# Routed mixture of experts: scale arithmetic from GpSimd to VectorE, a sequence prepared every six tile steps, the next tile's weight address read behind the present up product

## What is computed

```python
def _L1_ffn_ref(x, w_gate, w1, w3, w2):
    xt = x.reshape(-1, embed_dim)
    logits = xt @ w_gate                                # 8 experts
    top_logits, sel = jax.lax.top_k(logits, 2)
    probs = jax.nn.softmax(top_logits, axis=-1)
    h = silu(einsum('td,edh->eth', xt, w1)) * einsum('td,edh->eth', xt, w3)
    y = einsum('eth,ehd->etd', h, w2)                   # H = 256
    yk = y[sel.T, t_idx[None, :], :]                    # the two chosen experts of each token
    return einsum('ktd,tk->td', yk, probs)
...
x = x + _L1_ffn_ref(_layernorm(x), w_gate, w1, w3, w2)
```

## Time and profile before

| | before |
|---|---|
| median of 3 runs | 2675.16 us (2672.88 to 2677.55) |
| the profiled execution's own time | 2669.71 us |
| its span, first to last instruction | 2667.5 us |
| granted TensorE clock, mean | 0.894 |
| busy: PE, DVE, ACT, POOL | 2200.5 (82%), 1647.1 (62%), 1278.4 (48%), 1448.1 us (54%) |
| the two routed layers | from about 1545 to 1845, and from 2364 to 2667.5 us of the span |

### The profile page before, as it was taken

How to read it: one execution, slowest core, us unless ns; L and a number is a source line. 1 busy time by engine, 2 the same in 40 slices (tenths; PEclk the granted TensorE clock), 3 DMA queues, 4 the chain that set the end, 5 groups by cost and what they waited for, 6 DMA issues and landing times. The chain is left out here.

```text
span 2667.5 us, 40619 instructions
## 1 busy us (share of the span) xinstructions
PE 2200.5 (82%) x11840; PEld 1315.8 (49%) x11840; DVE 1647.1 (62%) x4376; ACT 1278.4 (48%) x2252; POOL 1448.1 (54%) x1499
## 2 busy tenths in 40 slices
PE   4577997998779889989999945776999999954766
PEld 3345564666656556644444433544444444433544
DVE  6865775776667657756666633435787787733424
ACT  4642454332435433336666523432677677642433
POOL 5923654443256533446666655744676666535743
PEclk8687898998979999989999957887999999966888
DMA  1001111222011122210000032232000000021224
GB/s 49 0 3 29 37 37 50 83 86 82 1 41 37 25 90 96 88 62 1 1 1 1 1 89 62 59 92 79 0 1 1 1 0 1 1 77 51 67 69 133
DMA packets 106948, 112.44 MB, mean 42 GB/s; under 512 B 21816, under 2 KB 86200, under 8 KB 106488
## 3 DMA queue, kind: packets, MB, share of 16 engines
q1 hardware_dynamic: 97656, 91.08, 11.6%
q0 software_dynamic: 9088, 18.89, 2.2%
HBM read 71.91 MB, written 25.29 MB: 36 GB/s over the span
## 5 line engine op out<-in xcount | busy, mean ns | idle before, releaser
L2330 DVE TENSOR_REDUCE l_diffneg_max<-psum 128x1 fp32r<-128x512 f32 x512 | 335.5, 685 | 92.7 <-PE psum L2068 86.6
L2245 ACT ACTIVATE l_diffweights<-psum 128x1024 f32<-128x1024 f32 x256 | 262.0, 1026 | 128.9 <-PE psum L2097 127.9
L2068 PE MATMUL psum<-l_diffkz,l_diffQ 128*128 128x512 f32 (+1 forms) x512 | 235.2, 478 | 3.2 <-DVE l_diffneg_max L2330 2.1
L5034 POOL DMA_INDIRECT results<-l_moe1y,l_moe1xt x156 | 151.8, 973 | 149.1 <-DVE l_moe1y L4944 129.6
L2869 ACT ACTIVATE l_lightswapped<-psum 32x512 f32<-32x512 f32 x304 | 179.0, 589 | 101.1 <-DVE l_lightturned L2961 97.7
L1595 DVE TENSOR_REDUCE l_attn0neg_max<-psum 128x1 fp32r<-128x512 f32 x256 | 167.2, 683 | 54.0 <-PE psum L1329 51.3
L4710 PE MATMUL psum<-l_moe1w,l_moe1zt 128*128 x312 | 186.2, 681 | 9.1 <-ACT l_moe1zt L4790 6.3
L1501 ACT ACTIVATE l_attn0weights<-psum 128x1024 f32<-128x1024 f32 x128 | 130.2, 1023 | 120.7 <-PE psum L1351 120.6
L174 POOL TENSOR_TENSOR settled<-powers 128x1 f32<-128x1 f32 x113 | 27.5, 244 | 294.1 <-DVE l_alibimv L701 69.6
L1722 POOL TENSOR_TENSOR l_attn0half_sums<-l_attn0weights 128x2048 f32<-128x2048 f32 x30 | 137.1, 4571 | 89.6 <-ACT l_attn0weights L1501 89.6
L4294 ACT ACTIVATE l_moe0s<-psum 128x512 f32<-128x512 f32 x144 | 85.8, 596 | 198.4 <-PE psum L854 173.9
(11 more groups left out here) (606 smaller groups left out, 6109.8 us busy)
## 6 DMA issues: line engine op xcount, KB each, us to landing
l_moe0bcs<-gate_rows SPq DMA_DIRECT2D x64, 512.0 KB, 4.4
l_moe1xt<-sorted SPq DMA_DIRECT2D x156, 66.0 KB, 1.8
l_attn0Q<-l_attn0q_hi SPq DMA_DIRECT2D x128, 64.0 KB
l_moe1yb<-results SPq DMA_DIRECT2D x32, 256.0 KB, 3.3
l_moe1w<-in_moe_w SPq DMA_DIRECT2D x6, 1024.0 KB, 8.3
l_attn0Q<-l_attn0q_lo SPq DMA_DIRECT2D x64, 64.0 KB
l_moe0w_raw<-in_moe_w SPq DMA_DIRECT2D x20, 128.0 KB, 4.7
results<-l_moe1y,l_moe1xt POOLq DMA_INDIRECT x156, 2.2
```

The source lines that it names most:

```text
L2068: nc.tensor.matmul(ps[:, bank, :], Q[rows, n % 4, st * P:(st + 1) * P], kz[rows, n % 4, hh, :], start=True, stop=True).then_inc(pe_max.sem ...
L2245: nc.scalar.activation(weights[:, tt, 2 * pair:2 * pair + 2, :], ps[:, S[m % 2]:S[m % 2] + 2, :], ACT.Exp, scale=SCALE).then_inc(act_exp.s ...
L2330: nc.vector.tensor_reduce(neg_max[:, n % 2, st, row:row + 1], ps[:, bank_of(("max", n, b)), :], AXX, ALU.max, negate=True).then_inc(vec_ma ...
L5034: p.indirect_dma_start(core.dram["results"], bass.IndirectOffsetOnAxis(ap=xt[:, n % SLOTS, R.DEST:R.DEST + 1].bitcast(U32), axis=0), y[:, ...
```

## The change

- `APART` is 6 in place of 8: a sequence every six steps. The chunk's sizes become tuples, with the same values (4 and 4 sequences), and loops over them are rewritten; a last empty turn is dropped.
- GpSimd's `token_scale` keeps the power only. VectorE adds epsilon to the variance behind the statistics (with a settling memset ahead) and makes the shift in a step of its own (`shifted`); variance, scale and shift get two buffers each. Sequence 0 takes the scale that the layer before left (`open_scale`) without GpSimd.
- `destinations` goes from GpSimd's two iotas per sequence to one iota for all at the layer's start and a cast on VectorE in `weighted`.
- On TensorE the address of tile i + 1 is read behind `up` of tile i.

```diff
-    SEQS = 4
...
+    SEQS = (4, 4)
...
-    APART, SPAN = 8, 10
+    APART, SPAN = 6, 10
...
-        TURNS = range(R.TILES + 3)
+        prepare_steps = lambda c: range(APART * (R.SEQS[c] - 1) + SPAN + 4)
+        turns = lambda c: range(R.TILES[c] + 2)
...
-                at_w = {}
+                at_w = {0: expert_of(0)}
                 tile_turned(n0)
                 tile_turned(n0 + 1)
-                for i in TURNS:
-                    if i < R.TILES:
-                        at_w[i] = t.value_load(table[0:1, c, W_AT + i:W_AT + i + 1], min_val=0, max_val=7 * R.COLS)
+                for i in turns(c):
+                    if i < R.TILES[c]:
                         up(n0 + i, at_w[i])
-                    if 0 <= i - 2 < R.TILES:
+                    if i + 1 < R.TILES[c]:
+                        at_w[i + 1] = expert_of(i + 1)
+                    if 0 <= i - 2 < R.TILES[c]:
                         down(n0 + i - 2, at_w.pop(i - 2))
...
             def tokens(j):
                 act_z.start()
-                wait(a, pool_scale, j, "shift")
+                wait(a, vec_shift, j, "shift")
                 if j >= 2:
                     rows_sorted(a, j - 2)
...
+                wait(d, vec_stats, j, "mean", NQ - 1)
+                settle(core, d)
+                wait(d, pool_scale, j - 2, "scale")
+                inc(v.tensor_scalar(var[:, j % 2, :], mv[:, j % 2, :, 1], LN_EPS, None, ALU.add), "var")
+
+            def shifted(j):
+                vec_shift.start()
+                if j:
+                    wait(d, pool_scale, j, "scale")
+                wait(d, act_z, j - 2, "again")
+                v.scalar_tensor_tensor(shift[:, j % 2, :], moments(j)[:, :, 0], -1.0, scale_of(j)[:, :], ALU.mult, ALU.mult
+                                       ).then_inc(vec_shift.sem, vec_shift.step("shift"))
...
+                inc(v.tensor_copy(rows[:, j % 2, :, :, R.DEST].bitcast(U32), dest[:, :, j, :]), "to")
...
+                if due(c, k, 1) is not None:
+                    shifted(due(c, k, 1))
...
+            nc.gpsimd.iota(dest[:, :, :, :].rearrange("p k j q -> p (k j q)"), [[P, 2 * NSEQ * NQ]], 0, 1).then_inc(counted, 1)
...
             def token_scale(j):
                 pool_scale.start()
...
-                if j:
-                    wait(p, vec_stats, j, "mean", NQ - 1)
-                wait(p, act_z, j - 1, "again")
-                settle(core, p)
-                inc(nc.gpsimd.tensor_scalar(minus[:, :], moments(j)[:, :, 0], -1.0, None, ALU.mult), "minus_mean")
-                inc(nc.gpsimd.tensor_scalar(var[:, :], moments(j)[:, :, 1], LN_EPS, None, ALU.add), "var")
-                wait_for("var")
-                inc(nc.gpsimd.tensor_tensor(scale[:, :], var[:, :], core.half, ALU.pow), "scale")
-                wait_for("scale")
-                inc(nc.gpsimd.tensor_tensor(shift[:, :], minus[:, :], scale[:, :], ALU.mult), "shift")
...
+                wait(p, vec_stats, j, "var")
+                wait(p, vec_shift, j - 2, "shift")
+                wait(p, act_z, j - 2, "again")
+                nc.gpsimd.tensor_tensor(scale[:, j % 2, :], var[:, j % 2, :], core.half, ALU.pow
+                                        ).then_inc(pool_scale.sem, pool_scale.step("scale"))
```

More of the change, by code:

```diff
@@ L13 @@
 from contextlib import ExitStack
+from itertools import accumulate
 import math
@@ L4554, in routed_block @@
         stats, mv = sb("stats", [P, NQ, 6]), sb("mv", [P, 2, NQ, 2])
-        minus, var, scale, shift = sb("minus", [P, NQ]), sb("var", [P, NQ]), sb("scale", [P, NQ]), sb("shift", [P, NQ])
+        var, scale, shift = sb("var", [P, 2, NQ]), sb("scale", [P, 2, NQ]), sb("shift", [P, 2, NQ])
         rows = sb("rows", [P, 2, 2, NQ, R.WIDTH])
@@ L4562, in routed_block @@
         count, whole, tiles_i, tiles, ends = sb("count", [P, 8]), sb("whole", [P, 8], I32), sb("tiles_i", [P, 8], I32), sb("tiles", [P, 8]), sb("ends", [P, 8])
[L4563 to L4566, removed]
+        passed, passed_tiles = sb("passed", [P, R.MOST, 8]), sb("passed_tiles", [P, R.MOST, 8])
+        expert, before = sb("expert", [P, R.MOST]), sb("before", [P, R.MOST])
+        at, at_row = sb("at", [P, R.MOST]), sb("at_row", [P, R.MOST])
+        table, dest = sb("table", [P, R.CHUNKS, PAD_AT + 8], I32), sb("destinations", [P, 2, NSEQ, NQ], I32)
         spare = sb("spare", [P, 8 + R.SPARES, R.WIDTH])
@@ L4572, in routed_block @@
         opening = core.opening
[L4573 removed]
+        for of in (vec_stats, pool_scale, pe_tr, act_hi, vec_lo):
             of.skip_first()
@@ L4577, in routed_block @@
         moments = lambda j: core.open_mv if j == 0 else mv[:, j % 2, :, :]
-        ROW_AT, W_AT, PAD_AT = 0, 40, 80
+        scale_of = lambda j: core.open_scale if j == 0 else scale[:, j % 2, :]
         def due(c, k, after):
             j, rest = divmod(k - after, APART)
-            return c * R.SEQS + j if rest == 0 and 0 <= j < R.SEQS and c < R.CHUNKS else None
-        PREPARE = APART * (R.SEQS - 1) + SPAN + 4
-        TURNS = range(R.TILES + 3)
+            return R.FIRST[c] + j if c < R.CHUNKS and rest == 0 and 0 <= j < R.SEQS[c] else None
+        prepare_steps = lambda c: range(APART * (R.SEQS[c] - 1) + SPAN + 4)
+        turns = lambda c: range(R.TILES[c] + 2)
+        spare_turns = lambda c: [k for k in prepare_steps(c + 1) if k not in turns(c)] if c + 1 < R.CHUNKS else []
         def wait(engine, of, rep, *step):
@@ L4636, in all_results @@
             def all_results(c):
-                for n in range((c + 1) * R.TILES - YS, (c + 1) * R.TILES):
+                for n in range(R.FIRST_TILE[c] + R.TILES[c] - YS, R.FIRST_TILE[c] + R.TILES[c]):
                     result_out(sp, n)
```

157 lines of the change are left out of this document (79 added, 78 removed).

## The result

| | before | changed |
|---|---|---|
| median of 15 runs each, same chip | 2672.9 us (2666.5 to 2692.2) | 2661.2 us (2651.4 to 2672.4) |
| ratio to before | | 0.9943, 95% interval 0.9927 to 0.9960 |
| the profiled execution's own time | 2669.7 us | 2654.7 us |
| its span | 2667.5 us | 2652.8 us |
| granted clock, mean | 0.894 | 0.891 |

What follows compares the result with a forecast made beforehand. GpSimd was taken to bound the preparation and first chunk's tiles, TensorE to be busy 71 of 74 us in the second chunk. -6.0 + 6.0 - 7.0 = -7.0 us a layer, two layers -14: 2675.2 to 2661.2 us, range 2646 to 2677.

Steps and rivals of the forecast that it cites:

- First part: Preparation alone, each routed layer: GpSimd's power e every 13.0 us instead of 15.82, -6.0 us a layer.
- Second part: First chunk's tiles: tokens wait for scatters, GpSimd stalls 3.85 us twice, +6.0 us a layer.
- Third part: TensorE's address load behind the up product: 0.165 us less per gap in the second chunk, -7.0 us a layer in all.
- The sum: Both routed layers: -7.0 us each, -14 us in all, forecast 2661.2 us, chance 0.55.
- B: First chunk's tiles: the new wait does not bite, second part -1.8, sum -29, 2646 us; chance 0.13.
- C: TensorE: the load only moves, the down product takes over the lateness, third part 0, 2675 us; chance 0.18.
- D: First chunk's tiles: stalls of turns 14 and 20 are 9 us, not 3.85; +6, 2682 us; chance 0.10.
- E: VectorE's added short instructions block GpSimd, 16 sequences cost 10 us: -4, 2671 us; chance 0.04.

Runs made afterwards that it cites:

- Experiments 6: The change with three buffers of rows and row numbers in place of two, and a third semaphore: 2640.2 us, ratio to before 0.9858.
- 8: The change with its two buffers of rows, but ScalarE's step `tokens` of each sequence one turn later: 2643.3 us, ratio to before 0.9877.
- 9: The change with rings of 14 places and 8 products y instead of 10 and 4, two buffers of rows kept: 2646.1 us, ratio to before 0.9909.
- experiment 1: The kernel before with only TensorE's address load moved behind the up product: 2654.7 us, ratio to before 0.9919.
- experiment 4: The change with sequences eight steps apart again (`APART, SPAN = 8, 10`): 2665.7 us, ratio to before 0.9957.
- all three combinations: The change with rings 14 and 8 plus: tokens one turn later, 2636.7 us; three row buffers, 2635.1; three row buffers and SyncE waiting for all three semaphores, 2635.0.

## Why the prediction was right, and where it was not

**First part, -6.0 a layer: right.** The forecast first scatter (1556.90, left unmoved) came at 1559.60 with the iota 2.7 later; the forecast first e, 1.5 us earlier, came at 1568.24, where 1582.84 - 15.82 - 1.5 + 2.7 gives 1568.2. The cycle of 12.95 was 12.98 and 13.07, through the same chain: scatter, landing, tokens, e. The table's start came 6.1 us sooner. The last e, forecast 7.1 us sooner, came 7.1 sooner, and of that 1.0 was given back up to the cast, where 1.1 was forecast. The remaining 0.7 of the stage belongs to the load, which no longer stands ahead of the first product up: with the load put back, the stage is 0.66 and 0.55 longer.

**Second part, +6.0 a layer: right in kind and place, and near in size.** Measured +6.6 and +5.4 with the load's gain in it, +6.8 and +8.6 without. Two stalls of 3.85 were forecast at turns 16 and 22: 4.26 and 4.73 came. From the result of turn 10 to the last copy 90.0 us were forecast, 90.6 measured; the start of turn 10 is unmoved (28.4 us behind the first product up in both), where 0.4 us later in this part and 0.7 sooner in the third had been forecast. Experiments 6 and 8 take the stalls away by two different means, 9 leaves them and takes the tail.

**Third part, -7.0 a layer: the term that was mis-sized.** I took "1.73 on late tiles and a little better on others", that is 0.165 less per gap, and left 1.63 as the upper bound. The measured pitch is that bound, 1.63 on nearly every tile, and the second chunk alone gave 8.8 and 9.2 us where I had 6.3. The step that failed was to think that the up product would go on waiting for its weights in late tiles: with the load gone from in front of them, and nothing else changed, this wait vanished nearly whole (27.9 us to 2.5, in experiment 1 as in the change). The prediction also weighed the queue of TensorE, to which the Trainium skill, TensorE: Matmul & The Clock Gate, section on the architectural detail of the array, gives a depth of 64. From that it inferred, which the page does not state, that the queue would cover the load and moving it would gain nothing; experiment 1, which moves only the load, shows 0.8%. The measurement decides: whatever the queue's depth, on 76 of 156 tiles the weights had to wait for issue while the load stood there.

**The sum.** -14 was forecast, the profiled spans differ by 14.7, the ratio says 15.2 (10.7 to 19.5). In the traces the two layers gained 19.8, and 5.1 was lost outside of them, 4.7 in code that is the same in both kernels and 0.4 in the drain. That the median fell on the forecast to 0.02 us is luck. The forecast was tied to the first 3 runs of before (2675.2), and the median of all 15 is 2672.9, so the medians differ by 11.7 and not by 14; and the two layers gained nearly 6 us more than forecast, most of it in the undersized third term, of which the loss outside took back all but 0.7.

**The rivals.** B (no stall): the idle times are there. C (the load only moves): refuted by experiment 1. D (stalls of 9 us): they are 4.3 and 4.7, and no 5 more. E (VectorE blocks GpSimd): in the timelines the scatters into `sorted` keep their 0.96 us (median of 128, of which one takes more than 1.1; before the change eight did) and their pitch of 1.26 beside VectorE's work.

## What to carry to other kernels

Ask of every wait that a change brings closer how many instructions the producer still has to issue, how long the last takes to land, and what stands behind the waiting instruction on its own engine; here moving one step of ScalarE by one turn gave back more than the new spacing had cost. A small address load in TensorE's instruction stream was best put behind the long product here, whose own inputs are ready, and a second one there was already too much. When two parts of a schedule change their distance, list which steps now fall together and in which order they are written (experiment 4).

## What the runs showed of the hardware that was not expected

TensorE's sequencer was nearly a bound of its own: an address read once a tile behind the product up, 0.65 us with the register work, leaves the products 1.63 us apart and the array without idle time between them; read twice, it costs 0.56 us a tile.

The granted clock fell at the end of layer 8, which no experiment touches, in some profiled executions and not in others. Windows from 2270 to 2340 us of the change with three buffers, and of the same with the ring of eight (columns as in the earlier trace rows):

```profile
2270.00:2300.00 30.00, 29.16 (x175) 12.49 (x167) 23.93 (x42) 21.96 (x27) 21.38 (x23) 1.00 0.00 1
2300.00:2320.00 20.00, 17.99 (x110) 8.30 (x108) 14.75 (x41) 11.39 (x13) 0.04 (x1) 1.00 0.01 2
2320.00:2340.00 20.00, 15.97 (x107) 6.56 (x108) 3.97 (x17) 13.21 (x16) 0.97 (x1) 0.99 0.00 1
```

```profile
2270.00:2300.00 30.00, 28.76 (x168) 12.35 (x165) 24.68 (x43) 22.48 (x28) 20.33 (x23) 1.00 0.00 1
2300.00:2320.00 20.00, 19.33 (x89) 8.25 (x89) 10.74 (x19) 7.79 (x10) 0.00 (x0) 0.67 0.01 2
2320.00:2340.00 20.00, 19.90 (x76) 6.56 (x76) 4.97 (x30) 11.56 (x14) 1.02 (x1) 0.50 0.00 0
```

TensorE was busy 29 of 30 us at full clock in both, and then got 2.4 GHz in the one and 1.2 in the other. From layer 7's last product up to layer 9's iota the first took 539.8 us, the second 549.5. The trace of the change itself shows full clock there. The change at eight steps, with tokens later, with each address read twice, and all three combinations show a fall (to between 0.50 and 0.59 in a window of 20 us); what decides it stays open. It is one reason why a stage's gain in a trace need not show in the time: the ring's 5 us over three buffers are half of such a fall.
